# A gated attention and expert block on one core: V projected ahead of the value products, small products moved to another PSUM bank

## Chip, cores and metric

One core of a Trainium2 chip runs the whole kernel, in one launch. The metric is device time in microseconds (us) of an execution; lower is better.

## What is computed

The reference, cut to what matters (8 batches of 256 tokens, width 128, 512 context rows, 16 heads of 64, 8 experts of 160 places):

```python
# attention part, on a layer-normed x
q = (xn @ w_q);  k, v = split(context @ w_kv)          # 16 heads of 64
attn = softmax(einsum('bqhd,bkhd->bhqk', q * SCALE, k))
out = einsum('bhqk,bkhd->bqhd', attn, v) @ w_out + b_out
x = x + tanh(g_xattn) * out * tanh(gate)
# expert part, on a layer-normed x: the best expert of each token, first come first served
logits = tokens @ gate_w;  probs = softmax(logits);  expert_idx = argmax(probs)
pos = cumsum(one_hot(expert_idx)) - 1                  # place within the expert, 160 at most
x = x + tanh(g_ffn) * combine(relu(expert_input @ w1) @ w2)
```

## The kernel before

The attention runs in 64 **slots**, one for each pair of heads: 8 batches b of 8 pairs hp, j = 8b + hp. Each engine has its own program in order; semaphores tie them together. In a slot j the engines do the following.

- **PE (TensorE)**: `scores` of pair j for two tiles of 128 queries (the first into bank pair psAB, the second into psCD; lines 1241 or 1234), `k_project` and `q_project` of pair j+2 (into psEF, lines 1168 to 1170), `o_transposes` of pair j-3 (line 1278), one *small product* in most slots, `values` of pair j-2 (into psO, lines 1267 to 1269), and `v_project` of one group of V (into psX, the same lines 1168 to 1170). In the slot hp = 2 `v_project` stands ahead of `values`, and the transposes of the next batch's context (line 1186, into psX) come last.
- **DVE (VectorE)**: row maximum of the first score tile (line 903, then the short 906), the low half of V (`v_lo`, line 896), row maximum of the second tile, the low half of K and Q of pair j+2 (`kq_lo`, line 890 or 886), then what reads the small product of this slot where that is an output product (`add_part`, line 947, in hp = 1; `add_attention`, line 936, in hp = 3), then `normalise_heads` of pair j-2 (lines 914 and 920, out of psO).
- **ACT (ScalarE)**: `exps` of the first tile (line 752), high half of K and Q (`kq_hi`, line 714), `phi` of the first tile (line 762, the high half of the probabilities), `exps` of the second, `ot_copy` (line 741), `phi` of the second, and the high half of V (`v_hi`, line 719).
- **POOL (GpSimd)**: the low half of the probabilities (line 650), two for a slot, and small steps of the normalisations and the routing.
- **SP's DMA queue**: two transposing DMAs for a slot (line 473), from PARTS to PT, which `values` reads two slots later.

The small products are: `ranks` in hp = 0 (of the batch before last), `project_part` in hp = 1 and `project` in hp = 3 (the two halves of the output projection of the batch before: 16 matmuls each, lines 1319 and 1355), `x_transposes` of the next batch in hp = 4 (line 1365), `tok_transposes` in hp = 5 (line 1286) and `logits` in hp = 6 (line 1294). All of them go to psX, and `wait_x` makes each writer of psX wait for the reader of the one before it; V's groups are among these writers. The readers of the x and token transposes are copies on ACT (lines 696 and 724), the others are on DVE. psO holds the value products alone; they wait for `norm_done` of the values before.

A split K/Q pair is done on ACT first (`kq_hi` waits for `q_project`) and then on DVE (`kq_lo` waits for `kq_hi`). After the last slot a tail follows: the last pairs' values, the routing of the last batch and the expert stage.

Of the kernel before, what the change touches and what calls it, by code (L numbers as in the profile page):

```python
# [33 lines left out]
def gated_block(nc, x, ctx_1024, g_xattn, g_ffn, ln_gamma, ln_beta, w_q, w_kv, w_out, b_out, gate,  # L34
# [34 lines left out]
    with ExitStack() as ctx:  # L69
# [123 lines left out]
        ps_logits = psX[:, 0:QT * E]  # L193
        ps_ranks = psX[:, 0:(QT + 1) * E]
        ps_gw_mid = psX[:, 0:E]
# [187 lines left out]
        def x_bank(b):  # L383
            return psX[:, 0:SQ] if b else psO
# [299 lines left out]
        def _(act):  # L684
# [5 lines left out]
            def xt_copy(b):  # L690

                act.wait_ge(xt_psum, b + 1)
                if b:

                    act.wait_ge(xt_lo_done, b)
                act.activation(XS[:], x_bank(b)[:, 0:SQ], ACT.Identity, bias=norm_q[:, 1:2],
                               scale=norm_q[:, 0:1]).then_inc(xt_f32, 1)
# [84 lines left out]
            def batch(b):  # L782
                for j, hp in slots(b):
# [56 lines left out]
        def _(dve):  # L840
# [33 lines left out]

            def ctxt_lo(b):
# [48 lines left out]
            def add_attention(b, banks=None):  # L924
# [11 lines left out]
                dve.scalar_tensor_tensor(out=x_of(b), in0=psX[:, 0:QT * D].rearrange("p (q d) -> p q d", q=QT),  # L936
# [4 lines left out]
            def add_part(b, part, bank=psX):  # L941
# [31 lines left out]
            def choose(b):  # L973

                n = b * ROUTE
                lg = ps_logits.rearrange("p (t e) -> p t e", e=E)
# [9 lines left out]
                dve.wait_ge(route, n + 4)  # L986
# [24 lines left out]
            def place(b):  # L1011


                n = b * ROUTE
                ranks = ps_ranks.rearrange("p (t e) -> p t e", e=E)
                dve.wait_ge(pos_psum, b + 1)
                dve.tensor_tensor(rank_hot[:], ranks[:, 0:QT, :], hot, ALU.mult).then_inc(route, 1)
                dve.tensor_copy(taken[:], ranks[:, QT, :]).then_inc(route, 1)
                dve.wait_ge(lexp_done, b + 1)
# [32 lines left out]
            def batch(b):  # L1052
                for j, hp in slots(b):
# [6 lines left out]
                    row_max(b, hp, 1)  # L1060
# [10 lines left out]
                    if hp == LOGITS_STEP and is_last(b):  # L1071
                        choose(b - 1)
# [29 lines left out]
            add_part(B - 1, B - 1)  # L1102
# [5 lines left out]
            choose(B - 1)  # L1108
            mark_first(B - 1)
            tokens(B - 1)  # L1110
            place(B - 1)
# [54 lines left out]
        def _(pe):  # L1166
# [14 lines left out]

            def ctx_transposes(b):
# [62 lines left out]
            def values(b, hp):  # L1245
# [35 lines left out]
            def tok_transposes(b, bank=psX):  # L1281
                if bank is psX:
                    wait_x((tokt_done, b + 1))
# [5 lines left out]
            def logits(b):  # L1289
                wait_x((route, b * ROUTE + 4))  # L1290
                pe.wait_ge(tokt_done, b + 1)
                pe.wait_ge(gw_mid_done, 1)
                for q in range(QT):
                    last = pe.matmul(ps_logits[:, E * q:E * q + E], tT[:, P * q:P * q + P], gw_mid[:], start=True, stop=True)
                last.then_inc(logit_psum, 1)

            def router_weights():

                wait_x((gw_mid_done, 1))
# [11 lines left out]
            def project_part(b, pairs, bank=psX):  # L1311

                if bank is psX:
# [9 lines left out]
            def ranks(b):  # L1323


                wait_x((route, b * ROUTE + 7))
# [6 lines left out]
                pe.matmul(ps_ranks.rearrange("p (t e) -> p t e", e=E), ident[:], carried, start=True, stop=False)  # L1333
                for i, (counts, c) in enumerate(((tri, 2), (ones_bf, 1), (ones_bf, 0))):
                    last = pe.matmul(ps_ranks, counts[:], hot_padded[:, c:c + QT + 1, :].rearrange("p t e -> p (t e)"),
# [13 lines left out]
            def project(b):  # L1349
                wait_x((x1_done, b + 1))  # L1350
                pe.wait_ge(ot_done, b * PAIRS + PAIRS)
                for qt in range(QT):
                    dst = psX[:, D * qt:D * qt + D]
# [6 lines left out]
            def x_transposes(b):  # L1360
                if b:
                    wait_x((xt_f32, b + 1))
# [23 lines left out]
            v_project(0, 0, 1, psO)  # L1386

            def batch(b):
                for j, hp in slots(b):
# [4 lines left out]
                    scores(b, hp, 1)  # L1394
                    if ahead:
# [9 lines left out]
                    if hp == RANKS_STEP and b > 1:  # L1405
                        ranks(b - 2)
                    if j == LAST:
                        ranks(b - 1)
                    if hp == PART_STEP and not is_first(b):
                        project_part(b - 1, range(PAIRS // 2))  # L1410
                    if hp == CTX_STEP:
                        v_project(*v_group(b, hp))
                    if hp == PROJECT_STEP and not is_first(b):
                        project(b - 1)
                    if hp == X_STEP and not is_last(b):
                        x_transposes(b + 1)
                    if hp == TOKT_STEP and not is_first(b):
                        tok_transposes(b - 1)
                    if hp == LOGITS_STEP and is_first(b):
                        router_weights()  # L1420
                    if hp == LOGITS_STEP and not is_first(b):
                        logits(b - 1)
# [4 lines left out]
                    if hp != CTX_STEP and v_group(b, hp):  # L1427
# [128 lines left out]
```

## Time and profile before

| | us |
|---|---|
| runs (median of 3; lowest, highest) | 475.88; 473.37, 476.15 |
| profiled execution, first to last instruction | 473.7 |
| busy: PE, ACT, DVE, POOL | 439.7, 386.4, 360.3, 356.6 |

The profiled execution has a span of 473.7 us, which is close to the lowest of the three runs and 2.2 us under their median; no other time of it is known, so the span stands for it. Busy times are sums over instructions, with the ends of matmuls modelled. What follows is read from the rows, where PE is TensorE's matmuls, PEld its weight loads, and a bracket `[0.90 <-PE psO L1269]` says how long the engine had been idle and what released it.

### The profile page before, as it was taken

How to read it: one execution, taken by the hardware profiler on the slowest of the kernel's cores; microseconds unless marked ns; L12 is line 12 of the kernel's file. 1: busy time of each engine (PE TensorE's matmuls, PEld its weight loads, DVE VectorE, ACT ScalarE, POOL GpSimd, SP SyncE). 2: the span in 40 equal slices, each digit the busy share in tenths (PEclk: the TensorE clock that was granted, in tenths of full speed). 3: DMA queues.
4: the chain of work that ended last, by engine and by line, in shares of the span. 5: the costliest groups of instructions: out<-in, count | busy, mean ns of one | idle time of the engine just before them, and what ended most of it. 6: DMA issues, size and time to landing. Idle time of an engine off the chain costs nothing.

```text
span 473.7 us, 13155 instructions
## 1 busy us (share of the span) xinstructions
PE 439.7 (93%) x5096; PEld 334.0 (71%) x5096; DVE 360.3 (76%) x789; ACT 386.4 (82%) x630; POOL 356.6 (75%) x270
## 2 busy tenths in 40 slices
PE   7889799998999989999999999999999999988993
PEld 6656667776767767776777667776777677758892
DVE  4787687778877887779787796878877887785622
ACT  5889788899888988899888898899799998892330
POOL 3687686888788887888878877898878877871325
PEclk9999999999999999999999999999999999999998
DMA  5499999999999999999999999999989998996021
GB/s 167 150 177 192 206 187 175 170 181 204 188 176 188 210 194 180 192 192 192 198 189 197 189 196 191 185 200 209 190 157 185 193 180 147 159 182 137 14 67 46
DMA packets 283037, 82.10 MB, mean 173 GB/s; under 512 B 264387, under 2 KB 280435, under 8 KB 282976
## 3 DMA queue, kind: packets, MB, share of 16 engines
q1 hardware_dynamic: 281600, 77.96, 93.4%
q0 software_dynamic: 1376, 3.30, 2.2%
q8 instruction: 41, 0.67, 0.6%
q14 instruction: 20, 0.16, 0.1%
HBM read 10.83 MB, written 5.14 MB: 34 GB/s over the span
## 4 chain that ended last, share of the span: by engine, by line
PE 40%; DVE 20%; ACT 16%; DMA 10%; issue 8%; POOL 4%; POOLq 0%; SPq 0%; ACTq 0%; DVEq 0%
DVE MXL L903 9%; DMA PT<-PARTS 9%; ACT P L752 7%; DVE HL L890 4%; ACT HL L714 4%; PE psAB L1234 3%; PE psX L1319 3%; PE psAB L1241 3%; PE psO L1267 3%; ACT PARTS L762 3%; POOL PARTS L650 3%; PE psX L1355 3%; DVE VL L896 3%; PE psO L1269 3%; PE psO L1268 3%
## 5 line engine op out<-in xcount | busy, mean ns | idle before, releaser
L650 POOL TENSOR_TENSOR PARTS<-P,PARTS 128x1024 f16<-128x1024 f32 x125 | 267.4, 2145 | 63.5 <-ACT PARTS L762 61.8
L762 ACT ACTIVATE PARTS<-P 128x1024 f16<-128x1024 f32 x126 | 136.1, 1080 | 0.7
L752 ACT ACTIVATE P<-psAB,NB 128x512 f32<-128x512 f32 x128 | 81.6, 695 | 41.8 <-DVE NB L906 41.4
L903 DVE TENSOR_REDUCE MXL<-psAB 128x2 f32<-128x1024 f32 x64 | 78.4, 1224 | 41.4 <-PE psAB L1241 23.9
L1267 PE MATMUL psO<-VH,PT 128*128 128x65 f16 x1008 | 98.6, 194 | 8.3 <-DMA PT<-PARTS 7.7
L1267 PEld LDWEIGHTS psO<-VH,PT 128*128 128x128 f16 x1008 | 92.0, 98 | 12.0 <-DMA PT<-PARTS 8.9
L1268 PE MATMUL psO<-VL,PT 128*128 128x64 f16 x1008 | 98.5, 192 | 0.0
L1269 PE MATMUL psO<-VH,PT 128*128 128x65 f16 x1008 | 98.4, 193 | 0.0
L1268 PEld LDWEIGHTS psO<-VL,PT 128*128 128x128 f16 x1008 | 91.3, 98 | 0.5
L1269 PEld LDWEIGHTS psO<-VH,PT 128*128 128x128 f16 x1008 | 91.5, 97 | 0.0
L752 ACT ACTIVATE P<-psCD,NB 128x512 f32<-128x512 f32 x128 | 81.7, 703 | 0.1
L903 DVE TENSOR_REDUCE MXL<-psCD 128x2 f32<-128x1024 f32 x64 | 77.8, 1215 | 0.2 <-PE psCD L1241 0.2
L896 DVE TENSOR_TENSOR VL<-psX,VH 128x512 f16<-128x512 f32 x63 | 43.1, 685 | 8.3 <-ACT VH L719 8.2
L890 DVE TENSOR_TENSOR HL<-psEF,HL 128x768 fp32r<-128x768 f32 x41 | 39.2, 957 | 5.8 <-ACT HL L714 2.5
L1241 PE MATMUL psCD<-HL 64*128 64x512 f32 x252 | 37.3, 400 | 4.7 <-ACT P L752 4.6
L1241 PE MATMUL psAB<-HL 64*128 64x512 f32 x252 | 40.5, 426 | 0.8 <-ACT P L752 0.8
L719 ACT ACTIVATE VH<-psX 128x512 f16<-128x512 f32 x63 | 39.3, 623 | 0.6 <-PE psX L1170 0.6
L741 ACT ACTIVATE OT<-psEF 128x256 f32<-128x256 f32 (+1 forms) x63 | 26.1, 414 | 10.7 <-PE psEF L1278 7.2
L1168 PEld LDWEIGHTS psEF<-cT_hi,w_hi 128*128 128x128 f32 x63 | 11.7, 186 | 31.9 <-issue 30.8
L714 ACT ACTIVATE HL<-psEF 128x768 fp32r<-128x768 f32 x41 | 33.3, 813 | 0.9 <-PE psEF L1170 0.7
L1241 PEld LDWEIGHTS psCD<-HL 64*128 64x128 f32 x252 | 22.8, 184 | 14.2 <-ACT P L752 9.7
L1168 PE MATMUL psEF<-cT_hi,w_hi 128*128 128x512 f32 x63 | 31.5, 500 | 1.0 <-DVE cT_lo L877 1.0
(214 smaller groups left out, 871.7 us busy)
## 6 DMA issues: line engine op xcount, KB each, us to landing
ctx_raw<-in_ctx_dram SPq DMA_DIRECT2D x8, 256.0 KB, 3.7
w1s<-in_L_ffn_w_dram SPq DMA_DIRECT2D x8, 256.0 KB, 3.6
w2s<-in_L_ffn_w_dram SPq DMA_DIRECT2D x8, 256.0 KB, 4.0
PT<-PARTS SPq DMA_TRANSPOSE x126, 5.0
experts_table<-zeros POOLq DMA_DIRECT2D x2, 645.0 KB, 4.0
X<-in_x_dram SPq DMA_DIRECT2D x8, 128.0 KB, 4.2
wraw<-in_L_xattn_w_kv_dram SPq DMA_DIRECT2D x4, 256.0 KB, 5.3
out_dram<-row SPq DMA_DIRECT2D x8, 128.0 KB, 2.5
```

The source lines that it names most:

```text
L650: pool.tensor_tensor(PARTS[:, par, qt, 1], P32[:, par, qt], PARTS[:, par, qt, 0], ALU.subtract).then_inc(plo_done, 1)
L714: act.activation(HL[:, hp % 2, H_KHI:H_KHI + KQ], kq_bank(j)[:, 0:KQ], ACT.Copy).then_inc(kq_hi_done, 1)
L752: last = act.activation(P32[:, par, qt, SK * h:SK * h + SK], score_bank(qt)[:, SK * h:SK * h + SK], ACT.Exp, bias=NB[:, par, qt, h:h + 1])
L762: act.activation(PARTS[:, hp % 2, qt, 0], P32[:, hp % 2, qt], ACT.Copy).then_inc(phi_done[qt], 1)
L890: dve.tensor_tensor(hl[:, H_KLO:H_KLO + KQ], kq_bank(j)[:, 0:KQ], hl[:, H_KHI:H_KHI + KQ].bitcast(F32), ALU.subtract).then_inc(kq_done, 1)
L896: dve.tensor_tensor(VL[:, kt, 8 * half:8 * half + 8, :], bank[:].rearrange("p (h d) -> p h d", d=DH), VH[:, kt, 8 * half:8 * half + 8, 0:D ...
L903: dve.tensor_reduce(MXL[:, par, qt, :, 0], score_bank(qt)[:].rearrange("p (h n) -> p h n", h=2), AX.X, ALU.max, negate=True).then_inc(max_ ...
L1168: pe.matmul(dst, hi_l, hi_r, start=True, stop=False)
L1241: last = pe.matmul(score_bank(qt)[:, SK * h:SK * h + SK], hl[rows, q + P * qt:q + P * qt + P], hl[rows, k:k + SK], start=(q == H_QHI and k ...
L1267: pe.matmul(psO[:, g:g + DH + 1], phi, VH[:, kt, head, 0:DH + 1], start=first_, stop=False)
L1268: pe.matmul(psO[:, g:g + DH], phi, VL[:, kt, head, :], start=False, stop=False)
L1269: last = pe.matmul(psO[:, g:g + DH + 1], plo, VH[:, kt, head, 0:DH + 1], start=False, stop=last_)
```

## The change

All small products of the slots go to psO in place of psX, and right behind the second scores, ahead of K, Q and everything else; V is projected ahead of the value products in every slot. A new chain `wait_o` orders the writers of psO: a small product waits for `norm_done` of the values of the slot before, and `values` waits for the reader of the small product of its own slot. The two copies that ACT did out of psX in the slots (x and token transposes) go to DVE, ahead of the second row maximum, as does the first part of `choose` and of `place`. On ACT `v_hi` moves ahead of the second `phi`. The tail keeps psX.

```diff
         def x_bank(b):
-            return psX[:, 0:SQ] if b else psO
+            return psO[:, 0:SQ]
@@ ACT, each slot
-                    if hp == X_STEP and not is_last(b):
-                        xt_copy(b + 1)
-                    if hp == TOKT_STEP and not is_first(b):
-                        tokt_copy(b - 1)
                     if j < LAST:
                         phi(b, hp, 0)
                     exps(b, hp, 1)
                     if ot_pair(j) >= 0:
                         ot_copy(ot_pair(j))
+                    if hp != CTX_STEP and v_group(b, hp):
+                        v_hi(*v_group(b, hp))
                     if j < LAST:
                         phi(b, hp, 1)
-                    if hp != CTX_STEP and v_group(b, hp):
-                        v_hi(*v_group(b, hp))
@@ DVE
+            def xt_copy(b):
+
+                dve.wait_ge(xt_psum, b + 1)
+                dve.wait_ge(norm_scaled, 1)
+                dve.wait_ge(xt_lo_done, b)
+                dve.tensor_scalar(XS[:], x_bank(b), norm_q[:, 0:1], norm_q[:, 1:2], ALU.mult, ALU.add)\
+                   .then_inc(xt_f32, 1)
+
+            def tokt_copy(b):
+
+                dve.wait_ge(tokt_psum, b + 1)
+                dve.tensor_copy(tT[:], psO[:, 0:QT * P]).then_inc(tokt_done, 1)
...
+            def take_ranks(b):
+
+                ranks = ps_ranks(b).rearrange("p (t e) -> p t e", e=E)
                 dve.wait_ge(pos_psum, b + 1)
                 dve.tensor_tensor(rank_hot[:], ranks[:, 0:QT, :], hot, ALU.mult).then_inc(route, 1)
                 dve.tensor_copy(taken[:], ranks[:, QT, :]).then_inc(route, 1)
@@ DVE, each slot
-                    row_max(b, hp, 1)
+                    if hp == RANKS_STEP and b > 1:
+                        take_ranks(b - 2)
+                    if hp == X_STEP and not is_last(b):
+                        xt_copy(b + 1)
+                    if hp == TOKT_STEP and not is_first(b):
+                        tokt_copy(b - 1)
                     if hp == LOGITS_STEP and is_first(b):
                         dve.wait_ge(gw_mid_psum, 1)
                         dve.tensor_copy(gw_mid[:], ps_gw_mid).then_inc(gw_mid_done, 1)
-                    if hp == LOGITS_STEP and not is_first(b) and not is_last(b):
+                    if hp == LOGITS_STEP and not is_first(b):
                         choose(b - 1)
+                    if j == LAST:
+                        take_ranks(B - 2)
+                    row_max(b, hp, 1)
+                    if hp == LOGITS_STEP and not is_first(b):
+                        first_winner(b - 1)
                     if hp == RANKS_STEP and b > 1:
                         place(b - 2)
@@ PE
+            o_free = [None]
+
+            def wait_o(free_when):
+
+                if o_free[0]:
+                    pe.wait_ge(*o_free[0])
+                o_free[0] = free_when
@@ PE, values
-                if j:
-                    pe.wait_ge(norm_done, turn(j) - 1)
-                else:
+                wait_o((norm_done, turn(j)))
+                if j == 0:
                     pe.wait_ge(row_consts, 1)
@@ PE, project_part (and in the same way project, with x1_done)
+                if bank is psO:
+                    wait_o((part_done, b + 1))
+                elif bank is psX:
                     wait_x((part_done, b + 1))
@@ PE, each slot
                     scores(b, hp, 1)
+                    if hp == RANKS_STEP and b > 1:
+                        ranks(b - 2)
+                    if j == LAST:
+                        ranks(b - 1)
+                    if hp == PART_STEP and not is_first(b):
+                        project_part(b - 1, range(PAIRS // 2))
+                    if hp == PROJECT_STEP and not is_first(b):
+                        project(b - 1)
+                    if hp == X_STEP and not is_last(b):
+                        x_transposes(b + 1)
+                    if hp == TOKT_STEP and not is_first(b):
+                        tok_transposes(b - 1)
+                    if hp == LOGITS_STEP and is_first(b):
+                        router_weights()
+                    if hp == LOGITS_STEP and not is_first(b):
+                        logits(b - 1)
                     if ahead:
...
                         o_transposes(ot_pair(j))
...
-                    if hp == CTX_STEP:
+                    if v_group(b, hp):
                         v_project(*v_group(b, hp))
...
                     if VALUES_BEHIND <= j < LAST:
                         values(*back(b, hp, VALUES_BEHIND))
                     if hp == CTX_STEP and not is_last(b):
                         ctx_transposes(b + 1)
-                    if hp != CTX_STEP and v_group(b, hp):
-                        v_project(*v_group(b, hp))
```

On DVE `kq_lo`, `add_part`, `add_attention` and `normalise_heads` keep their order behind the second row maximum.

## Rows read from the trace of the kernel before

**Rows 1.** The page: the chain that ended last, by engine.

```profile
PE 40%; DVE 20%; ACT 16%; DMA 10%; issue 8%; POOL 4%; POOLq 0%; SPq 0%; ACTq 0%; DVEq 0%
```

**Rows 2.** Windows by slot, batch 3, hp 1, 3, 4; length, busy times, PEclk, DMA.

```profile
176.70:184.08 7.38, 7.32 (x88) 5.98 (x87) 6.29 (x12) 6.99 (x12) 5.89 (x5) 1.00 1.14 195
...
190.97:198.23 7.26, 7.26 (x88) 5.99 (x87) 5.25 (x11) 6.81 (x12) 6.90 (x5) 1.00 1.17 186
198.23:204.13 5.90, 5.88 (x74) 4.46 (x73) 5.35 (x14) 4.34 (x8) 4.25 (x5) 1.00 1.23 171
...
sum 51.08, PE 50.09 PEld 37.50 DVE 41.89 ACT 44.64 POOL 41.74; mean PE 6.26 PEld 4.69 DVE 5.24 ACT 5.58 POOL 5.22
```

**Rows 3.** Timeline of PE, slot b = 3, hp = 1: start, length, instruction.

```profile
176.70 0.97 PE L1241 MATMUL psAB<-HL 64*128 64x512 f32 x6
...
178.29 0.50 PE L1168 MATMUL psEF<-cT_hi,w_hi 128*128 128x512 f32 x1
...
179.10 0.28 PE L1168 MATMUL psEF<-xT_hi,w_hi 128*128 128x256 f32 x1
...
179.45 0.38 PE L1278 MATMUL psEF<-ident,O 128*128 128x128 f32 x2
179.88 2.05 PE L1319 MATMUL psX<-wo,OT 128*128 128x128 f32 x16
...
181.77 0.19 PE L1267 MATMUL psO<-VH,PT 128*128 128x65 f16 x1
...
183.21 0.48 PE L1168 MATMUL psX<-w_hi,cT_hi 128*128 128x512 f32 x1
...
184.08 0.70 PE L1234 MATMUL psAB<-wraw 64*128 64x512 f32 x2
```

**Rows 4.** Timeline of DVE and ACT, the same slot.

```profile
179.14 0.69 DVE L896 TENSOR_TENSOR VL<-psX,VH 128x512 f16<-128x512 f32 x1
...
181.16 0.96 DVE L890 TENSOR_TENSOR HL<-psEF,HL 128x768 fp32r<-128x768 f32 x1
182.04 0.48 DVE L947 SCALAR_TENSOR_TENSOR X<-psX,gscale,X 128x256 f32<-128x256 f32 x1
183.41 0.18 DVE L914 RECIPROCAL rden<-psO 128x4 f32<-128x4 f32 x1 [0.90 <-PE psO L1269]
183.63 0.42 DVE L920 TENSOR_TENSOR O<-psO,rden 128x256 f32<-128x256 f32 x1
...
180.32 0.81 ACT L714 ACTIVATE HL<-psEF 128x768 fp32r<-128x768 f32 x1
```

**Rows 5.** Timeline of DVE from the end of hp = 3 into hp = 4.

```profile
197.57 0.18 DVE L914 RECIPROCAL rden<-psO 128x4 f32<-128x4 f32 x1 [0.79 <-PE psO L1269]
...
199.31 1.23 DVE L903 TENSOR_REDUCE MXL<-psAB 128x2 f32<-128x1024 f32 x1 [0.30 <-PE psAB L1241]
...
200.65 0.68 DVE L896 TENSOR_TENSOR VL<-psX,VH 128x512 f16<-128x512 f32 x1
```

**Rows 6.** Waits over the whole run: waiter, releaser, us in total, times, longest.

```profile
PEld psO L1267 <- DMA PT<-PARTS: 8.9, 9, 2.6
...
PEld psX L1294 <- DVE VL L896: 2.4, 7, 1.3
...
PEld psX L1319 <- DVE VL L896: 2.0, 7, 0.3
...
PEld psX L1365 <- DVE VL L896: 1.8, 7, 0.3
PEld psX L1286 <- DVE VL L896: 1.6, 7, 0.2
```

**Rows 7.** Timeline around the last slot: DVE's second row maximum, POOL's marks.

```profile
423.65 1.22 DVE L903 TENSOR_REDUCE MXL<-psCD 128x2 f32<-128x1024 f32 x1
...
423.06 0.60 POOL L600 TENSOR_SCALAR hot_padded<-iota_e,place 128x8 bf16<-128x8 f32 x2
```

**Rows 8.** Windows at the wait of hp = 7, b = 2; columns as in rows 2.

```profile
166.73:168.46 1.73, 0.89 (x26) 0.76 (x24) 1.58 (x3) 1.73 (x4) 1.69 (x4) 1.00 1.55 99
```

More of the change, by code:

```diff
@@ L191, in gated_block, with ps_logits, ps_ranks @@
         psX = pb("psX", [P, 512])
-        ps_logits = psX[:, 0:QT * E]
-        ps_ranks = psX[:, 0:(QT + 1) * E]
-        ps_gw_mid = psX[:, 0:E]
+        def ps_logits(b):
+            return (psX if b == B - 1 else psO)[:, 0:QT * E]
+        def ps_ranks(b):
+            return (psX if b == B - 1 else psO)[:, 0:(QT + 1) * E]
+        ps_gw_mid = psO[:, 0:E]
         x_in = sem("x_in")
@@ L935, in add_attention, with add_part @@
                     return
-                dve.scalar_tensor_tensor(out=x_of(b), in0=psX[:, 0:QT * D].rearrange("p (q d) -> p q d", q=QT),
+                dve.scalar_tensor_tensor(out=x_of(b), in0=psO[:, 0:QT * D].rearrange("p (q d) -> p q d", q=QT),
                                          scalar=gscale[:, 0:1], in1=X1[:, bass.ds(b * QT, QT), :], op0=ALU.mult,
                                          op1=ALU.add).then_inc(x1_done, 1)
-            def add_part(b, part, bank=psX):
+            def add_part(b, part, bank=psO):
                 dve.wait_ge(part_psum, part + 1)
@@ L1018, in place @@
                 dve.tensor_copy(taken[:], ranks[:, QT, :]).then_inc(route, 1)
+            def place(b):
+                n = b * ROUTE
                 dve.wait_ge(lexp_done, b + 1)
@@ L1101, in _ @@
             normalise_heads(B - 1, PAIRS - 3)
-            add_part(B - 1, B - 1)
+            add_part(B - 1, B - 1, psX)
             normalise_heads(B - 1, PAIRS - 1)
@@ L1108, in _ @@
             choose(B - 1)
+            first_winner(B - 1)
             mark_first(B - 1)
             tokens(B - 1)
+            take_ranks(B - 1)
             place(B - 1)
@@ L1279, in o_transposes, with tok_transposes @@
                 last.then_inc(ot_psum, pairs)
-            def tok_transposes(b, bank=psX):
-                if bank is psX:
-                    wait_x((tokt_done, b + 1))
+            def tok_transposes(b, bank=psO):
+                if bank is psO:
+                    wait_o((tokt_done, b + 1))
                 pe.wait_ge(x1_done, B - 1 + QT if is_last(b) else b + 1)
@@ L1289, in logits @@
             def logits(b):
-                wait_x((route, b * ROUTE + 4))
+                (wait_x if b == B - 1 else wait_o)((route, b * ROUTE + 4))
                 pe.wait_ge(tokt_done, b + 1)
@@ L1293, in logits @@
                 for q in range(QT):
-                    last = pe.matmul(ps_logits[:, E * q:E * q + E], tT[:, P * q:P * q + P], gw_mid[:], start=True, stop=True)
+                    last = pe.matmul(ps_logits(b)[:, E * q:E * q + E], tT[:, P * q:P * q + P], gw_mid[:], start=True, stop=True)
                 last.then_inc(logit_psum, 1)
             def router_weights():
-                wait_x((gw_mid_done, 1))
+                wait_o((gw_mid_done, 1))
                 pe.wait_ge(gw_in, 16)
@@ L1309, in last_transposes, with project_part @@
                 last.then_inc(p_psum, 1)
-            def project_part(b, pairs, bank=psX):
-                if bank is psX:
+            def project_part(b, pairs, bank=psO):
+                if bank is psO:
+                    wait_o((part_done, b + 1))
+                elif bank is psX:
                     wait_x((part_done, b + 1))
@@ L1323, in ranks @@
             def ranks(b):
-                wait_x((route, b * ROUTE + 7))
+                (wait_x if b == B - 1 else wait_o)((route, b * ROUTE + 7))
                 pe.wait_ge(hot_done, QT * (b + 1))
@@ L1349, in project @@
             def project(b):
-                wait_x((x1_done, b + 1))
+                wait_o((x1_done, b + 1))
                 pe.wait_ge(ot_done, b * PAIRS + PAIRS)
                 for qt in range(QT):
-                    dst = psX[:, D * qt:D * qt + D]
+                    dst = psO[:, D * qt:D * qt + D]
                     for pair in range(PAIRS // 2, PAIRS):
@@ L1435, in batch @@
                     values(b, PAIRS - 3)
-                    project_part(b, range(PAIRS // 2))
+                    project_part(b, range(PAIRS // 2), psX)
                     values(b, PAIRS - 1)
```

35 lines of the change are left out of this document (7 added, 28 removed).

## The prediction

> **What bounds the kernel now.** I read the page first, then the windows by slot, then the timeline of one slot on each engine, and the list of waits last. The page gives TensorE 40% of the chain that ended last [rows 1], which alone does not say that it is the bound. The windows by slot do: of the 51.08 us of batch 3, TensorE is busy in 50.09, and the slot with the first output product in it (hp = 1) is full to 7.32 of 7.38 us [rows 2]. In the timeline of that slot each group of matmuls starts where the group before it ends: from its first scores at 176.70 to those of the next slot at 184.08 there is no hole [rows 3]. So a slot is as long as TensorE's list of work, plus what TensorE waits for. The waits are short and of two kinds: small products that wait until VectorE has emptied psX of V (2.4, 2.0, 1.8 and 1.6 us for the four costliest of them), and value products that wait for their transposing DMA (8.9 us in 9 places) [rows 6]. Every other engine has a tenth or more to spare in the batch [rows 2]. What the change is worth is therefore read from TensorE: which waits go, and which new ones appear.
>
> **The durations that I use**, all from the slot hp = 1 [rows 3]: both score tiles 1.59 (176.70 to 178.29), K 0.81 (178.29 to 179.10), Q 0.35 (179.10 to 179.45), the transposes of O 0.2 (0.43 to the next product, of which the wait on psX is 2.0/7 = 0.29 [rows 6], so between 0.14 and 0.21 as the split goes), the output product 1.89 (179.88 to 181.77), the value products 1.44 (181.77 to 183.21), V 0.87 (183.21 to 184.08). From the other engines [rows 4]: from the start of ScalarE's high half to VectorE's low half 0.84 (180.32 to 181.16), from there to the addition of the product 0.88 (181.16 to 182.04), the addition 0.48 and some 0.05 for its signal. Q's last matmul ends some 0.5 after Q's start (three of 0.28, 0.12 apart), so ScalarE can start 0.55 after it.
>
> **Slots hp = 1 and hp = 3: the new wait.** The moved output product now stands ahead of K and Q, and its reader on VectorE still stands behind the low half of K and Q. So the reader waits for K and Q, which wait for the product: scores 1.59 + product 1.89 + K 0.81 = 4.29 until Q starts, + 0.55 = 4.84 ScalarE's high half, + 0.84 = 5.68 VectorE's low half, + 0.88 = 6.56 the addition, + 0.53 = 7.09 psO is free. TensorE meanwhile does scores, product, K, Q, the transposes and V: 1.59 + 1.89 + 0.81 + 0.35 + 0.2 + 0.87 = 5.71, and then asks for psO to write the value products there. It stands still for 7.09 - 5.71 = **1.38 us**. The product's own wait, for the normalisation of the values before, costs nothing: that starts 1.64 - 1.44 = 0.2 after the first scores (181.77 to 183.41 [rows 3, 4]) and lasts 0.64 (183.41 to 183.63 + 0.42 [rows 4]), and the scores hide it until 1.59. Before, nothing of the longer wait was on the path: the values had psO to themselves, and V behind them needed psX only at 183.21, when the addition (182.04 + 0.48) had long ended [rows 3, 4]. The slot becomes 7.09 + 1.44 = 8.53 in place of 7.38: +1.15, in 7 batches +8.0. The slot hp = 3 has the same order with `add_attention` in place of `add_part`, an operation of the same shape: 8.53 in place of 7.26 [rows 2], +1.27, in 7 batches +8.9. What is queued behind VectorE's late addition is the normalisation of the same slot, which needs the values that wait for it, so it adds no more in hp = 1.
>
> **Slot hp = 4: a knock-on.** Values are now the last thing TensorE does in a slot, so the normalisation ends 0.87 later against the next scores. After hp = 3 that matters, because the token moments come behind it. From the start of the values to the normalisation is 1.64 (181.77 to 183.41 [rows 3, 4]), from there to the first row maximum 1.74 and to V's low half 1.34 more [rows 5], and 0.74 from that to a free psX (179.14 to 179.88 [rows 3, 4]): 5.46 from the start of the values, which is 5.46 - 1.44 = 4.02 after the first scores of hp = 4. TensorE is ready for V there after 1.59 + 0.3 (x transposes, a pair like that of O) + 0.81 + 0.35 + 0.2 = 3.25. It waits 0.77, and the slot is 4.02 + 0.87 + 1.44 = 6.33 in place of 5.90 [rows 2]: +0.43 in six batches; in the last batch, which has no x transposes, that slot is shorter and loses about 1.0. Sum +3.6.
>
> **What the change takes away.** The waits on psX end. Those of hp = 1, 3 and 4 are already inside the slot lengths above; left are the logits' 2.4 and the token transposes' 1.6 [rows 6]: -4.0, with 0 and -6 as bounds (TensorE may regain some 0.1 of pipelining per slot as well).
>
> **Edits costed at nothing.** The copies of x and token transposes leave ScalarE and go to VectorE ahead of the second row maximum. No row shows a VectorE copy of 256 columns out of psO alone; the nearest is the addition with the same 256 columns, 0.48 [rows 4], and below it a copy cannot cost less than nothing. I take 0.4: the second exponentials start up to 0.4 later, but ScalarE has given up a step of the same size, and the next reader, the second scores of the next slot, is more than a slot of other matmuls away. Without that cover it would be 0.4 x 14 = 5.6. `choose` ahead of the row maximum is alike. V's high half ahead of `phi` delays the second probabilities, POOL's low half and the transposing DMA behind it by half a microsecond, and in hp = 1 and 3 by a microsecond more; the values that read them come two slots later and, with V ahead, 0.87 further down the slot. I take both as equal: the 8.9 us of DMA waits [rows 6] stay. Bounds: all of them go (-8.9), or each batch gains another microsecond of them (+7).
>
> **The tail.** In the last slot `take_ranks` now stands ahead of the second row maximum. The ranks need POOL's marks, done at 423.06 + 0.60 = 423.66, then a product and its signal of some 0.5 (estimate, as for Q above) and two short reads; the row maximum began at 423.65 [rows 7]. It slips by about 0.8, with the last exponentials behind it: +0.8, between 0 and 1.
>
> **Sum**: 8.0 + 8.9 + 3.6 + 0.8 - 4.0 = +17.3; batch 0 has no output products and none of these losses, and its x transposes gain a little, which I round to -0.3: **+17.0**. Against the profiled span of 473.7 that is 490.7; the median of the three runs lies 2.2 higher, and the forecast on it is 475.9 + 17.0 = **492.9 us**, slower by 3.6%.
>
> **Rivals.**
> - *The bank is free in time* (the other side). If psO came free before TensorE asks for it, only the gains would be left: 7.8 us of psX waits (the four rows added up) and, with V as cover, perhaps half of the DMA waits, 4.4 [rows 6]: 475.9 - 12.2 = 464 us. It decides at 5.71 us into hp = 1 and 3: the addition would have to end 1.38 sooner, which it would if VectorE added ahead of the K/Q low half. The product itself ends at 3.5, so there is time for that; but the queue puts the addition behind, and the low half cannot start without Q. Chance 0.04.
> - *TensorE has slack that takes the waits up.* The weight loads fill only 37.50 of 51.08 us [rows 2]; if matmuls wait in the records for something else, an added wait is hidden, and the time stays within 1%, at 476. Against it: the groups follow without a hole [rows 3]. The Trainium skill ("Perfetto Trace Analysis", Identifying the Most-Contended Engine) holds matmul busy share to be a poor measure of distance from the limit and takes the weight loads' share instead; by that this rival would be the likelier one. The trace does not follow it here, since the starts of the groups, and not their modelled ends, fill the slot. Chance 0.06.
> - *The wait is met only in part* (the addition starts sooner than I chain it, or the knock-on of hp = 4 is absorbed): about half the loss of hp = 1 and 3 and no knock-on: 475.9 + 8.5 + 0.8 - 4.0 = 481 to 486 us. Chance 0.12.
> - *The transposing DMAs come later too*: +7 on the forecast, 500 us. Chance 0.11.
> - *The clock falls.* TensorE now stands still twice a batch for 1.4 us. In the trace it stood as long for the DMA at 166.73, and the granted clock was 1.00, 2.4 GHz, through it [rows 8]. Were it at 1.2 GHz in the following slot each time, the 5.88 busy us there [rows 2] would double: 14 x 5.9 = 82 us, 575. The Trainium skill ("TensorE: Matmul & The Clock Gate", A second HAM failure mode: psum-queue depth-cycling) says that short waits between groups on a PSUM queue can make the clock swing; by that this would be the result, and these rows speak against it. Chance 0.01.
>
> **From these to the numbers.** The forecast has the remaining 0.66. With the unknown cost of the DMA waits the forecast itself runs from 475.9 + 17.0 - 8.9 = 484 to 475.9 + 17.0 + 7 = 500; the partial case reaches below. The range 483 to 501 leaves out the first two rivals, the clock and part of the partial case, under 0.2 together. A change of 1% (4.8 us) is about what a measurement of this kernel can tell from none: faster 0.04, the same 0.07 (the slack and a sliver of the partial case), slower 0.89.
>
> **What the profile after would show.** Slots hp = 1 and hp = 3 of about 8.5 us, with the value products released by the addition (VectorE line of `add_part` or `add_attention`) after a wait of some 1.4 us; K's first matmul in them 1.9 us later than now; a wait of V on V's low half of some 0.8 in hp = 4; no wait of logits or token transposes on V. The prediction is wrong if the addition starts before ScalarE's high half ends, if the values wait less than 0.5 us for psO, or if slots hp = 5 to 7 lose their DMA waits altogether.

## The result, and the profile after

The changed kernel takes 489.79 us (median of 4 runs, 488.61 to 491.75) beside 475.98 us for the kernel before (4 runs): a ratio of 1.0324, 95% interval 1.0282 to 1.0366. It is slower by 13.8 us, where 17.0 was forecast (492.9, range 483 to 501). The profiled execution has a span of 487.9 us, against 473.7.

First the windows by slot, for the slots hp = 1, 3 and 4 of batch 3, with the columns of [rows 2].

```profile
177.20:186.01 8.81, 7.16 (x91) 5.97 (x88) 5.59 (x10) 7.09 (x13) 7.43 (x5) 1.00 1.05 181
192.89:201.68 8.79, 7.14 (x89) 5.95 (x89) 4.62 (x7) 7.06 (x13) 7.03 (x5) 1.00 1.15 172
201.68:207.69 6.01, 5.66 (x78) 4.37 (x75) 5.73 (x15) 3.80 (x6) 4.08 (x5) 1.00 1.15 175
```

The two slots with an output product have grown from 7.38 and 7.26 to 8.81 and 8.79 us, and TensorE, which filled them before, is idle in them for 1.65 us. The slot behind, hp = 4, went from 5.90 to 6.01. The granted clock is 1.00 in all three, and so it is in all 14 slots hp = 1 and 3 of batches 1 to 7.

The timeline of TensorE in the slot hp = 1 answers to [rows 3]: start, length, instruction, and in brackets how long the engine stood idle before it and what ended that.

```profile
177.20 0.97 PE L1274 MATMUL psAB<-HL 64*128 64x512 f32 x6
...
178.80 2.05 PE L1353 MATMUL psO<-wo,OT 128*128 128x128 f32 x16
180.60 0.47 PE L1193 MATMUL psEF<-cT_hi,w_hi 128*128 128x512 f32 x1
...
181.37 0.28 PE L1193 MATMUL psEF<-xT_hi,w_hi 128*128 128x256 f32 x1
...
181.74 0.38 PE L1310 MATMUL psEF<-ident,O 128*128 128x128 f32 x2
181.88 0.47 PE L1193 MATMUL psX<-w_hi,cT_hi 128*128 128x512 f32 x1
...
184.47 0.20 PE L1299 MATMUL psO<-VH,PT 128*128 128x65 f16 x1 [1.65 <-DVE X L957]
...
186.01 0.70 PE L1267 MATMUL psAB<-wraw 64*128 64x512 f32 x2
...
205.33 0.50 PE L1193 MATMUL psX<-w_hi,cT_hi 128*128 128x512 f32 x1 [0.35 <-DVE VL L906]
```

The list is as read from the code: scores, product (178.80), K (180.60), Q (181.37), the transposes of O (181.74), V (181.88), and then a hole of 1.65 us until the addition of line 957 has emptied psO. The last row is V of the slot hp = 4, which waits 0.35 us for V's low half. The timelines of ScalarE and VectorE in the same slot, and of VectorE at the start of hp = 4, answer to [rows 4, 5].

```profile
182.22 0.81 ACT L715 ACTIVATE HL<-psEF 128x768 fp32r<-128x768 f32 x1 [1.29 <-PE psEF L1310]
...
183.06 0.96 DVE L900 TENSOR_TENSOR HL<-psEF,HL 128x768 fp32r<-128x768 f32 x1 [1.51 <-ACT HL L715]
183.93 0.47 DVE L957 SCALAR_TENSOR_TENSOR X<-psO,gscale,X 128x256 f32<-128x256 f32 x1
186.11 0.18 DVE L924 RECIPROCAL rden<-psO 128x4 f32<-128x4 f32 x1 [1.71 <-PE psO L1301]
...
201.78 0.18 DVE L924 RECIPROCAL rden<-psO 128x4 f32<-128x4 f32 x1 [1.71 <-PE psO L1301]
...
203.26 1.22 DVE L913 TENSOR_REDUCE MXL<-psAB 128x2 f32<-128x1024 f32 x1
...
204.59 0.68 DVE L906 TENSOR_TENSOR VL<-psX,VH 128x512 f16<-128x512 f32 x1
```

The whole chain stands here as one wait behind the other: ScalarE idle for TensorE (1.29), VectorE idle for ScalarE (1.51), TensorE idle for VectorE (1.65). Before, ScalarE's high half began at 180.32 in a slot from 176.70, 3.62 in; now it begins 5.02 in.

The list of waits answers to [rows 6].

```profile
PEld psO L1299 <- DVE row L946: 14.6, 7, 2.1
PEld psO L1299 <- DVE X L957: 14.6, 7, 2.1
...
PEld psO L1299 <- DMA PT<-PARTS: 2.6, 6, 0.8
```

Two new rows, seven times each, one for `add_attention` and one for `add_part` (these are the weight loads; the last of them ends 0.4 us ahead of the last matmul before the hole, so their wait is 2.1 us beside the matmuls' 1.65); the row for the transposing DMA fell from 8.9 to 2.6; the rows of small products that waited for V's low half are gone. One new wait came where none was forecast: in hp = 6 of the last batch the values wait 1.16 us for VectorE's `winners` (line 994), the reader of the logits.

**Where the 14.2 us between the two spans lie**, by step: the distance from the first score row of a slot to that of the next, added over batches 1 to 7, before and after. hp = 1: 51.75 to 61.61 (+9.9). hp = 3: 51.62 to 62.50 (+10.9). hp = 4: 40.73 to 42.03 (+1.3). hp = 5 and 6: 85.18 to 81.06 (-4.1, of which hp = 5 has -2.9 and hp = 6 -1.2). hp = 7: 36.76 to 33.72 (-3.0). hp = 0 and 2: +0.3. Batch 0: 52.89 to 51.77 (-1.1). The stretch from the last slot's scores to the end: 52.55 to 53.18 (+0.6). Before the first scores: -0.5.

### The profile page after: what moved, and what is told of

It reads as the page before. It is cut to its first block, busy times and chain, and to the rows that moved or that the text cites. A ratio compares the mean times of both kernels' runs of the same rounds, so it can differ in the third digit from the quotient of the medians.

```text
span 487.9 us, 13156 instructions
## 1 busy us (share of the span) xinstructions
PE 433.6 (89%) x5096; PEld 334.3 (69%) x5096; DVE 367.0 (75%) x803; ACT 382.9 (78%) x616; POOL 355.7 (73%) x270
## 4 chain that ended last, share of the span: by engine, by line
PE 53%; DVE 18%; ACT 12%; DMA 7%; issue 6%; POOL 3%; POOLq 0%; SPq 0%; ACTq 0%; DVEq 0%
DVE MXL L913 7%; DMA PT<-PARTS 6%; PE psO L1299 5%; ACT P L753 4%; PE psAB L1267 4%; PE psO L1301 4%; ACT HL L715 4%; PE psO L1300 4%; PE psAB L1274 4%; PE psCD L1274 3%; DVE HL L900 3%; PE psEF L1193 3%; PE psO L1389 3%; PE psO L1353 3%; PE psEF L1195 2%
## 5 line engine op out<-in xcount | busy, mean ns | idle before, releaser
L924 DVE RECIPROCAL rden<-psO 128x4 f32<-128x4 f32 x64 | 11.4, 179 | 35.2 <-PE psO L1301 34.6
L1193 PE MATMUL psX<-w_hi,cT_hi 128*128 128x512 f32 x63 | 30.2, 479 | 5.0 <-DVE VL L906 2.6
L742 ACT ACTIVATE OT<-psEF 128x256 f32<-128x256 f32 (+1 forms) x63 | 25.1, 399 | 9.1 <-PE psEF L1310 7.2
L1274 PEld LDWEIGHTS psCD<-HL 64*128 64x128 f32 x252 | 22.5, 186 | 14.3 <-ACT P L753 10.2
```

Of the source, the lines that this page charges most:

```text
L1193: pe.matmul(dst, hi_l, hi_r, start=True, stop=False)
L1274: last = pe.matmul(score_bank(qt)[:, SK * h:SK * h + SK], hl[rows, q + P * qt:q + P * qt + P], hl[rows, k:k + SK], start=(q == H_QHI and k ...
```

## The experiments

Experiments 1 to 4 and 8 are the changed kernel with one edit each; 6 puts two of these edits together, 7 adds another to it, and 9 one more; the fifth edits the kernel before. None leaves out any work.

**1. Additions first.**

```diff
+                    if hp == PART_STEP and not is_first(b):
+                        add_part(b - 1, b - 1)
+                    if hp == PROJECT_STEP and not is_first(b):
+                        add_attention(b - 1)
                     if not (is_last(b) and hp + AHEAD >= PAIRS):
                         kq_lo(*next_pair(b, hp, AHEAD))
...
-                    if hp == PART_STEP and not is_first(b):
-                        add_part(b - 1, b - 1)
-                    if hp == PROJECT_STEP and not is_first(b):
-                        add_attention(b - 1)
```

> The changed kernel, with VectorE's two additions (add_part in hp = 1, add_attention in hp = 3) ahead of the low half of K and Q. If the loss is the values' wait for psO behind the chain product, K, Q, high half, low half, addition, that wait (1.65 us in the trace, 14 times) goes to nothing: slots hp = 1 and 3 of 7.15 us in place of 8.80, 14 x 1.65 = 23 less, 467 us. Rival: the loss comes from K and Q being late behind the product, whatever the addition does; then these slots stay above 8 us and the time above 480.

475.53 us, ratio to before 0.9995 (0.9957 to 1.0033): 14.3 us under the changed kernel, where 23 were expected. The wait is gone and the slots did what the theory says, hp = 3 shown here, and the rival, which kept them above 8 us, is out:

```profile
186.15:193.13 6.98, 6.98 (x89) 5.94 (x88) 4.66 (x7) 5.24 (x9) 5.22 (x5) 1.00 1.29 180
204.96:211.97 7.01, 6.01 (x79) 4.61 (x76) 5.34 (x13) 6.06 (x12) 6.24 (x5) 1.00 1.18 196
```

hp = 3 is full again at 6.98 us; over batches 1 to 7, hp = 1 and 3 together went from 124.1 to 99.9 us, -24.2. Of the 10 that are missing from that, 8 came back in hp = 6 and 7 (74.0 us over these batches in the changed kernel, 82.1 here): the second row is hp = 6, 7.01 us with TensorE idle for 1.0 of it (6.13 in the changed kernel's batch 3), and the waits name the transposing DMA:

```profile
PEld psO L1299 <- DMA PT<-PARTS: 9.5, 13, 2.1
```

Some 1.6 us of the 8 is not a wait: in hp = 7 of batch 5 (7.17 us in place of 5.59) the granted clock was down, behind a DMA wait of 1.95 us.

**2. Output products behind the transposes of O.** VectorE's order stays as changed.

```diff
-                    if hp == PART_STEP and not is_first(b):
-                        project_part(b - 1, range(PAIRS // 2))
-                    if hp == PROJECT_STEP and not is_first(b):
-                        project(b - 1)
...
                         o_transposes(ot_pair(j))
+                    if hp == PART_STEP and not is_first(b):
+                        project_part(b - 1, range(PAIRS // 2))
+                    if hp == PROJECT_STEP and not is_first(b):
+                        project(b - 1)
                     if v_group(b, hp):
                         v_project(*v_group(b, hp))
```

> The changed kernel, with the two output products back behind the transposes of O (still in psO, ahead of V); VectorE's order as changed. If the chain is the cause, K and Q are early again, the addition ends some 5.9 us into the slot and the values ask at 5.5: a wait of 0.2 to 0.5 is left, slots of 7.4 to 7.6 us, about 472 us. Rival: sharing psO between product and values is what costs, wherever the product stands; then the slots stay above 8 us and the time above 482.

472.05 us, ratio 0.9941 (0.9916 to 0.9966): as expected, and already 0.6% faster than the kernel before. The rest of the wait is in the timeline of hp = 1:

```profile
178.14 0.20 PE L1299 MATMUL psO<-VH,PT 128*128 128x65 f16 x1 [0.26 <-DVE X L957]
```

0.26 in place of 1.65, so sharing the bank costs little by itself, 3.6 us in 14 slots. What costs is the product ahead of K and Q together with its reader behind their low half: either edit, this one or that of experiment 1, takes the wait away or nearly so.

**3. Copies back on ScalarE.** `xt_copy` and `tokt_copy` run on ScalarE ahead of the first `phi`, out of psO.

```diff
+                    if hp == X_STEP and not is_last(b):
+                        xt_copy(b + 1)
+                    if hp == TOKT_STEP and not is_first(b):
+                        tokt_copy(b - 1)
                     if j < LAST:
                         phi(b, hp, 0)
```

> The changed kernel, with the copies of x and token transposes back on ScalarE, reading psO. The prediction took their move at nothing: 490 us within 2. Rival: on VectorE, ahead of the second row maximum, they delay the exponentials and cost 0.4 us each, 14 of them: 484 us with the copies back.

493.79 us, ratio 1.0406 (1.0352 to 1.0460): neither. Once the copies read psO, their place on VectorE is worth some 4 us (3.1 between the two spans). On ScalarE the copy stands behind the first exponentials and the high half of K and Q, and in hp = 4 the values wait for the bank until it is through (timeline of TensorE):

```profile
208.25 0.20 PE L1288 MATMUL psO<-VH,PT 128*128 128x65 f16 x1 [0.89 <-ACT XS L699]
```

hp = 4 takes 7.06 us in place of 6.01 in six batches, +6.3; hp = 5 wins 0.2 back in each, and with hp = 6 and batch 0 some 3 of the 6.3 come back.

**4. Values ahead of V.**

```diff
-                    if v_group(b, hp):
+                    if hp == CTX_STEP:
                         v_project(*v_group(b, hp))
                     if VALUES_BEHIND <= j < LAST:
                         values(*back(b, hp, VALUES_BEHIND))
                     if hp == CTX_STEP and not is_last(b):
                         ctx_transposes(b + 1)
+                    if hp != CTX_STEP and v_group(b, hp):
+                        v_project(*v_group(b, hp))
```

> The changed kernel, with the values ahead of V again in all slots but hp = 2. If the values wait for the bank, they ask 0.8 us earlier and get it at the same moment, and V comes behind: slots hp = 1 and 3 of 9.6 us, 14 x 0.8 = 11 to 12 more, 502 us; and if V ahead is what hid the waits for the transposing DMA, some of those come back as well (up to 9 more). Rival: the order of V and values does not matter to this loss: 490 us.

517.14 us, ratio 1.0889 (1.0828 to 1.0949): the theory's direction, 15 us beyond its 502 and 6 beyond the 511 with all of its DMA waits. The windows show why, a slot hp = 1 and then one of hp = 3, cut where its values start:

```profile
186.01:195.59 9.58, 7.24 (x89) 5.93 (x88) 6.20 (x12) 6.57 (x11) 6.88 (x5) 1.00 1.02 180
...
202.47:209.72 7.25, 4.90 (x37) 4.00 (x37) 4.62 (x7) 5.52 (x10) 5.48 (x5) 1.00 1.00 210
209.72:213.54 3.82, 3.82 (x52) 3.37 (x52) 0.94 (x5) 0.94 (x3) 1.72 (x1) 0.56 0.36 90
```

The first is the 9.6 us of the theory. In the second the granted clock is 0.56 behind the wait, which is now 2.35 us long: the values and V, which take 1.45 + 0.87 in the slot hp = 1, take 3.82. This is the clock rival of the prediction, in part of the slots and for part of a slot; six of the 14 show it (0.56 to 0.59, 3.67 to 3.87 us in place of 2.31), at some 1.5 us each, 9 us. The other eight, with the same wait, stay at 1.00. The DMA waits are back as well:

```profile
PEld psO L1299 <- DMA PT<-PARTS: 14.0, 17, 1.9
```

2.6 with V ahead, 14.0 with V behind: V's 0.8 us are the cover of the transposing DMA that the change was able to give.

**5. V ahead alone.** The kernel before, small products in psX.

```diff
+                    if v_group(b, hp):
+                        v_project(*v_group(b, hp))
                     if VALUES_BEHIND <= j < LAST:
                         values(*back(b, hp, VALUES_BEHIND))
...
-                    if hp != CTX_STEP and v_group(b, hp):
-                        v_project(*v_group(b, hp))
```

> The kernel before, with one part of the change alone: V ahead of the values in every slot, the small products left in psX and in their old place. Theory: V now asks for psX right behind the small product and waits until its reader is through, and the values wait behind V: the addition (some 0.9 us after V could start in hp = 1 and 3), the copies on ScalarE in hp = 4 and 5 and the choice in hp = 6 (0.7 each), about 4.5 us a batch and 505 us; the move to psO is what V ahead needs. Rival: V ahead alone costs nothing and hides the DMA waits: 468 us.

514.96 us, ratio 1.0820 (1.0774 to 1.0866): the theory, and more than it said. V waits for the small product's reader in six of the eight slots (0.5 to 1.4 us each), here in hp = 6:

```profile
230.86 0.50 PE L1168 MATMUL psX<-w_hi,cT_hi 128*128 128x512 f32 x1 [1.27 <-DVE winners L984]
```

With the small products left where they were, V ahead in every slot does need a second bank for them. In hp = 4 the wait is 1.42 us, and in two batches the granted clock fell behind it (slots of 8.69 and 9.31 us in place of 7.86).

**6. Products behind and additions first**: the edits of experiments 1 and 2 together.

> The changed kernel with both edits: the output products behind the transposes of O, and VectorE's additions ahead of the low half of K and Q. Theory: the rest of the wait in hp = 1 and 3 (0.4 us in 7.40) goes, slots of 7.0, 14 x 0.4 = 5 to 6 less than with the products behind alone, 467 us, if the waits for the transposing DMA stay near the 4 us of that run. These waits grew to 9 where K and Q are late (additions first, products early), since the first probabilities and with them POOL start 1.4 us later there; with K and Q early they should not. Rival: the DMA waits follow from shorter slots alone; then they grow to 9 again and the time stays at 472.

466.85 us, ratio 0.9834 (0.9798 to 0.9870): as the theory had it. Slots hp = 1 and 3 of about 7.03 us, as short as in experiment 1, but 8.7 us faster than that. The rival (shorter slots alone bring the DMA waits) is out as the whole cause; that shorter slots can bring them too is seen in experiment 7. The two kernels differ in when K and Q run, and the timelines of ScalarE and POOL at the end of hp = 3 show what hangs on that. Experiment 1 (slot from 186.15):

```profile
191.15 0.81 ACT L715 ACTIVATE HL<-psEF 128x768 fp32r<-128x768 f32 x1 [1.28 <-PE psEF L1310]
191.86 1.05 ACT L763 ACTIVATE PARTS<-P 128x1024 f16<-128x1024 f32 x1
...
192.99 2.15 POOL L654 TENSOR_TENSOR PARTS<-P,PARTS 128x1024 f16<-128x1024 f32 x1 [1.54 <-ACT PARTS L763]
```

Experiment 6 (slot from 184.38), and its DMA waits:

```profile
187.99 0.81 ACT L715 ACTIVATE HL<-psEF 128x768 fp32r<-128x768 f32 x1
188.68 1.07 ACT L763 ACTIVATE PARTS<-P 128x1024 f16<-128x1024 f32 x1
...
189.83 2.14 POOL L654 TENSOR_TENSOR PARTS<-P,PARTS 128x1024 f16<-128x1024 f32 x1
```

```profile
PEld psO L1299 <- DMA PT<-PARTS: 5.0, 7, 1.7
```

The first `phi` stands behind the high half of K and Q in ScalarE's queue: 5.71 us into the slot where Q is late, 4.30 where it is early, and POOL's low half follows (6.84 and 5.45). What is late in hp = 3 makes POOL's next low half late (2.71 us into hp = 4 in experiment 1, 1.28 in 6), and hp = 4 is what the values of hp = 6 read: hp = 6 and 7 are 82.1 us over batches 1 to 7 in experiment 1, and 74.8 in experiment 6 (one profile each).

**7. Token moments ahead of the normalisation** in hp = 3, on top of 6.

```diff
+                    if hp == PROJECT_STEP and not is_first(b):
+                        token_moments(b - 1)
                     if VALUES_BEHIND <= j < LAST:
                         normalise_heads(*back(b, hp, VALUES_BEHIND))
-                    if hp == PROJECT_STEP and not is_first(b):
-                        token_moments(b - 1)
```

> As the one before, with the token moments of hp = 3 ahead of the normalisation in place of behind it (they need the addition alone, and VectorE is idle there until the values end). Theory of the knock-on: in hp = 4 the wait of V for psX (0.35) and in hp = 5 that of the second scores for the exponentials (0.3) go, 0.6 to 0.7 in 6 batches, 4 us less than the one before: 463 us. Rival: the knock-on is not the moments' doing, and the time is that of the one before.

466.27 us, ratio 0.9813 (0.9773 to 0.9853): not to be told from experiment 6. The knock-on was the moments' doing, as the windows of hp = 4 show, and the gain went elsewhere, as those of hp = 6 show. hp = 4 and 6 of batch 3, experiment 6, then 7:

```profile
191.40:197.42 6.02, 5.67 (x76) 4.37 (x74) 5.74 (x15) 4.19 (x7) 4.46 (x5) 1.00 1.19 181
203.24:209.41 6.17, 5.85 (x78) 4.61 (x75) 5.34 (x13) 5.93 (x11) 6.14 (x4) 1.00 1.07 188
```

```profile
192.14:197.57 5.43, 5.43 (x76) 4.37 (x73) 5.02 (x10) 4.17 (x7) 4.43 (x5) 1.00 1.17 150
203.42:210.78 7.36, 6.00 (x78) 4.60 (x75) 5.33 (x13) 6.00 (x12) 6.09 (x4) 1.00 1.13 200
```

And the waits of experiment 7:

```profile
PEld psO L1299 <- DMA PT<-PARTS: 10.0, 11, 1.7
```

Over batches 1 to 7 hp = 4 lost 4.0 us, and hp = 6 and 7 gained 4.8, with K and Q as early as in experiment 6; the wait in hp = 5 for the exponentials stayed.

**8. The second `phi` ahead of V's high half**, in the changed kernel.

```diff
-                    if hp != CTX_STEP and v_group(b, hp):
-                        v_hi(*v_group(b, hp))
                     if j < LAST:
                         phi(b, hp, 1)
+                    if hp != CTX_STEP and v_group(b, hp):
+                        v_hi(*v_group(b, hp))
```

> The changed kernel, with V's high half on ScalarE behind the second phi again. The prediction took this part of the change at nothing. Theory: in hp = 2 to 7 V's high half comes 0.95 us later, V's low half waits for it and the second row maximum with it, some 0.3 to 0.5 us a slot, mostly hidden; the DMA waits are small here: 490 us within 3. Rival: with the second probabilities 0.5 us earlier POOL and the DMAs are ahead, and 2 to 3 us are won, 487 us.

489.04 us, ratio 1.0303 (1.0263 to 1.0343), on 1.0324 for the changed kernel: no difference that this measurement tells. The prediction's zero for this edit stands.

**9. The same edit on top of 7.**

> As the run with the moments ahead, with V's high half on ScalarE behind the second phi again. That run won 0.57 us in each hp = 4 and gave it back in waits for the transposing DMA (10 us in place of 5). If these waits come from late probabilities, phi 0.5 us earlier in hp = 3 to 7 takes some half of them back: 462 us. Rival: POOL itself, or the DMA, is the limit in hp = 3 to 6 (it works without a break there), and an earlier phi only waits for it: 466 us.

465.19 us, ratio 0.9799 (0.9760 to 0.9839), between what the two sides expected, and within the interval of experiments 6 and 7. The DMA waits are 7.1 in its profile, beside 10.0; one profile each, so the share of ScalarE and of POOL in them stays open. Kernels 6, 7 and 9 all beat both kernels of the case; 9 has the best median, 1.9% under the kernel before (474.08, run beside it).

## Why the prediction was right

**The new wait** is the cause, and it was forecast by name, place and size: predicted 1.38 us, 14 times; measured 1.65. Experiments 1 and 2 take it away from either end of its chain, and the slots shrink by what the wait was. One step of the chain was read wrongly from the code. The prediction lets ScalarE's high half start when Q is done, as the list of the slot's work says; `kq_hi` also waits for the transposes of O (`ot_psum`), which stand behind Q in TensorE's queue. So from Q's start to the high half it is 0.85 us (181.37 to 182.22) where 0.55 was taken: the two transposes end at 182.12, and ScalarE starts 0.10 later, in all 14 slots. In the kernel before ScalarE was still at its exponentials then, but for one slot, hp = 3 of batch 7, whose row shows the link:

```profile
400.56 0.81 ACT L714 ACTIVATE HL<-psEF 128x768 fp32r<-128x768 f32 x1 [0.20 <-PE psEF L1278]
```

The other links are as read: 0.84 to VectorE's low half (182.22 to 183.06), 0.87 to the addition, 0.54 to the values. Q itself starts 0.12 earlier than was added up (4.17 us into the slot, not 4.29), so the bank comes free 0.18 late, at 7.27 and not 7.09, and TensorE asks for it at 5.62 and not 5.71. The rest is the values, which take 1.54 us where the next scores follow them (184.47 to 186.01), not the 1.44 they took ahead of V. Both together make a slot of 8.81 in place of 8.53, and hp = 1 and 3 cost +20.7 in place of +16.9.

**The knock-on in hp = 4** was right in kind, which experiment 7 shows, and too large: V waits 0.35 us there, not 0.77, and the step gained 1.3 in place of 3.6. The term that was mis-sized most is the stretch from the normalisation to the row maximum. I took 1.74 from [rows 5], but that row says in its bracket that 0.30 of it was VectorE waiting for TensorE; without the wait it is 1.48 (201.78 to 203.26). The other 0.1 is again that of the values.

**The waits taken away**: hp = 5 and 6 lost 4.1 us, predicted 4.0, but not slot by slot: 2.9 and 1.2 where 1.6 and 2.4 were forecast, since the values of the last batch's hp = 6 now wait 1.16 us for the reader of the logits. That the sums agree is luck. The tail gave 0.6, predicted 0.8. Batch 0 gave -1.1, predicted -0.3.

**The DMA waits** were taken at no change, with -8.9 as the bound; they fell by 6.3, which is seen in the 3.0 us that hp = 7 lost and in the 2.7 of hp = 5 of batch 0 (8.39 to 5.67). In hp = 5 to 7, where the prediction named their total loss as a sign of being wrong, they went from 7.8 to 1.3. Experiment 4 shows V ahead as the reason for the larger part (2.6 with it, 14.0 without), and experiments 1 and 6 that late probabilities bring them back once the slots are short; that the long slots hide this in the changed kernel fits, and is not shown by itself.

**The total.** The spans differ by 14.2 us where 17.0 was forecast: the miss on hp = 1 and 3 (+3.8) and that on the knock-on (-2.3) leave +1.5, and hp = 7 (-3.0), batch 0 (-0.8 beyond its forecast) and the start (-0.5) are most of what takes it below. The wait that decides was rightly found; that the sum lies within 3 us is in part luck, since misses of up to 3.8 us stand on either side.

**The copies on VectorE** were costed at nothing, with 0.4 us each as the price if the cover were gone. Experiment 3 says that, with psO as their source, the move gains some 4 us: I had looked at who stands behind the copies in VectorE's queue and not at where they stand in ScalarE's, behind the exponentials, with a bank now waiting for them.

**The rivals.** *The bank is free in time* did not happen in the change, and needed just what the prediction named, the addition ahead of the low half; made so, it is worth 14 us and not the full 23. *TensorE has slack* is out: what weight loads leave free absorbed nothing: 1.65 us of new wait came into hp = 1, 0.29 of an old one went, and the slot is 1.43 longer. *The clock* stayed at 2.4 GHz behind the 1.65 us in all 14 slots of the profiled execution. The reason that was given for it is weak, though. The window of [rows 8] ends before the wait is over; the wait itself is this row of the kernel before, and a longer one in batch 0 would have said more:

```profile
169.15 0.20 PE L1267 MATMUL psO<-VH,PT 128*128 128x65 f16 x1 [1.53 <-DMA PT<-PARTS]
51.28 0.20 PE L1267 MATMUL psO<-VH,PT 128*128 128x65 f16 x1 [2.53 <-DMA PT<-PARTS]
```

The granted clock was 1.00 behind both. In other runs it fell behind waits as short as 1.42 us (last section), so that it stayed up here is what the profile shows and not something the prediction could know. One execution of the changed kernel without a profile has a mean granted clock of 0.985, beside 0.994 in the profiled one, so some falls there are possible.

## What to carry to other kernels

Moving a product forward does not free its bank earlier if its reader stays behind other work that the move has delayed: follow the reader's whole queue, read every semaphore that each step of it waits for, and move the two together or not at all. Here the best was the reader moved forward and the product left behind K and Q. When TensorE is the bound, cost a change slot by slot from the start times of its groups, and take a link from a row only after looking whether that row was waiting for something else. A stall removed from one slot can come back as a wait for data three slots on, where the engines that make the data had been using the stall as their own slack.

## What the runs showed of the hardware

TensorE's granted clock can fall to its lower level, 1.2 GHz, behind a wait of 2.35 us between two groups of a slot that was busy before and after (a mean of 0.56 over the next 3.82 us, experiment 4); in eight of the 14 slots with the same wait it stayed at 2.4 GHz, and behind the 1.65 us of the changed kernel it stayed there in all 14. The length of the wait does not tell the two apart in these runs. The clock also fell behind two of six waits of 1.42 us in experiment 5, behind waits of 1.59 us in batch 0 of experiments 1, 3 and 6, behind 1.95 us in experiment 1, and once in the changed kernel, in batch 0, behind 2.39 us; in the kernel before it stayed at 1.00 behind 2.53 us. Below are the row of a wait and the window behind it, first for the changed kernel (V and the values, which take 2.35 us in the same slot of experiment 2, at full clock behind a wait of 2.43 us), then for experiment 5:

```profile
37.12 0.50 PE L1193 MATMUL psX<-w_hi,cT_hi 128*128 128x512 f32 x1 [2.39 <-DVE cT_lo L887]
37.12:40.29 3.17, 3.17 (x52) 2.76 (x53) 2.19 (x3) 3.17 (x6) 0.80 (x1) 0.70 1.23 132
```

```profile
157.79 0.79 PE L1168 MATMUL psX<-w_hi,cT_hi 128*128 128x512 f32 x1 [1.42 <-ACT XS L696]
157.79:161.00 3.21, 3.21 (x35) 2.59 (x36) 0.48 (x1) 3.21 (x6) 2.13 (x1) 0.50 0.80 219
```

The Trainium skill ("TensorE: Matmul & The Clock Gate", A second HAM failure mode: psum-queue depth-cycling) describes a clock that swings between its two levels where TensorE idles briefly and often between groups on a PSUM queue. These traces agree in part: the falls stand behind single waits of 1.4 us and more, and most slots with such waits show none.

One small VectorE operation took 2.27 us in the changed kernel in place of 0.29 in the kernel before: the scaling of `bo` (128 by 128, fp32, in SBUF) in batch 0, hp = 3. V then waits 2.39 us for VectorE, the clock falls behind that wait, and the slot takes 8.68 us in place of 5.48 (hp = 5 won 2.7 of it back). The timelines of VectorE and POOL there, changed kernel, then kernel before:

```profile
31.80 1.03 DVE L1114 TENSOR_TENSOR gscale<-tgates 128x1 f32<-128x1 f32 x1
32.87 2.27 DVE L1117 TENSOR_SCALAR bo<-bo,gscale 128x128 f32<-128x128 f32 x1
...
30.68 4.38 POOL L654 TENSOR_TENSOR PARTS<-P,PARTS 128x1024 f16<-128x1024 f32 x2 [1.14 <-ACT PARTS L763]
```

```profile
33.69 0.29 DVE L1094 TENSOR_SCALAR bo<-bo,gscale 128x128 f32<-128x128 f32 x1
...
31.50 4.48 POOL L650 TENSOR_TENSOR PARTS<-P,PARTS 128x1024 f16<-128x1024 f32 x2 [1.49 <-ACT PARTS L762]
```

In all eleven traces the operation starts some 0.05 us behind the end of one of POOL's operations, just as the next is due. In two (the changed kernel and experiment 2) it ends with that next one, after 2.27 us. In the other nine it takes 0.29, and in eight of them POOL's next low half is the longer by some 0.1 us (2.23 to 2.25 in place of 2.14), which is the difference of 4.48 and 4.38. So the 2.27 us are not tied to the change; the rows show no reason why one or the other goes first. The Trainium skill ("Advanced Engine Details and Errata", VectorE Performance Modes, Mode Summary) says that GpSimd instructions and VectorE instructions that use both SBUF ports block each other; these rows agree with that, and no run here takes the two apart on purpose.
